# A state-space layer with a routed feed-forward block: moving sums, residual and rounding rest of a chunk from VectorE and GpSimd to TensorE and ScalarE, with new job orders

## The reference, cut to what matters

```
x = x + ssm(layernorm(x))
x = x + ffn(layernorm(x))
```

## Time and profile before

| | |
|---|---|
| median of three runs | 1964.43 us |
| lowest, highest | 1963.17, 1964.90 us |
| profiled execution, own time | 1968.13 us |
| its span, first to last instruction | 1966.3 us |
| VectorE busy | 1823.1 us (93%) |
| GpSimd busy | 1791.7 us (91%) |
| TensorE busy (matmuls) | 1628.6 us (83%) |
| ScalarE busy | 1431.6 us (73%) |
| mean granted clock of TensorE, share of full speed | 0.933 |

### The profile page before, as it was taken

One profiled execution on the slowest core, in us unless ns is written; L12 is line 12 of the kernel. 1 busy time (PEld: TensorE's weight loads), 2 busy tenths in 40 slices (PEclk: granted clock), 3 DMA queues, 4 the chain that ended last, 5 costly groups with the idle time before them and its releaser, 6 DMA issues.

```text
span 1966.3 us, 25727 instructions
## 1 busy us (share of the span) xinstructions
PE 1628.6 (83%) x6816; PEld 808.6 (41%) x6816; DVE 1823.1 (93%) x2246; ACT 1431.6 (73%) x2755; POOL 1791.7 (91%) x780
## 2 busy tenths in 40 slices
PE   3364779898898989889898988889898898988899
PEld 1111224444443444444344444444444444444456
DVE  2799999999999999999999999999999999999951
ACT  3566767877787777878777787877778787777643
POOL 1899999999999999999999999999999999999920
PEclk8666879999899999989999999999999999999999
DMA  4646553544646365464636536463643646265200
GB/s 167 142 112 155 119 138 90 142 123 92 161 111 155 91 152 123 96 151 112 161 84 149 126 92 152 112 165 79 158 118 94 148 111 166 68 156 118 58 14 19
DMA packets 146761, 234.92 MB, mean 119 GB/s; under 512 B 22064, under 2 KB 46896, under 8 KB 146096
## 3 DMA queue, kind: packets, MB, share of 16 engines
q1 hardware_dynamic: 146608, 233.18, 48.7%
HBM read 190.11 MB, written 42.99 MB: 119 GB/s over the span
## 4 chain that ended last, share of the span: by engine, by line
DVE 32%; POOL 23%; issue 17%; PE 17%; ACT 5%; DMA 1%; DVEq 0%; SPq 0%; POOLq 0%; ACTq 0%
POOL hs L1344 14%; DVE decay L1286 13%; DVE hs L1276 8%; DVE hs L1286 7%; POOL hs L1356 6%; PE bank L910 4%; PE bank L932 4%; ACT decay L1089 2%; PE y_ps L946 2%; POOL e_dt L1334 1%; DVE st L1146 1%; POOL z_dt L1323 1%; PE bank L894 1%; PE bank L914 1%; PE bank L884 1%
## 5 line engine op out<-in xcount | busy, mean ns | idle before, releaser
L1344 POOL TENSOR_TENSOR hs<-dx_rep,b_rep 128x2048 f32<-128x2048 f32 x256 | 1161.8, 4541 | 13.4 <-issue 11.1
L1286 DVE TENSOR_TENSOR_SCAN decay<-decay,state,hs 128x512 f32<-128x512 f32 x640 | 796.2, 1277 | 34.2 <-ACT decay L1089 27.4
L1089 ACT ACTIVATE decay<-dt_rep,a_sb 128x512 f32<-128x512 f32 x1024 | 690.0, 685 | 28.7 <-DMA dt_rep<-rep_scratch 10.3
L1286 DVE TENSOR_TENSOR_SCAN hs<-decay,state,hs 128x512 f32<-128x512 f32 x384 | 487.3, 1269 | 4.3 <-ACT decay L1089 3.7
L1356 POOL TENSOR_TENSOR hs<-hs,c_rep 128x1024 f32<-128x1024 f32 x192 | 453.6, 2362 | 6.3 <-ACT state L1103 6.3
L1276 DVE TENSOR_TENSOR hs<-decay,c_rep 128x1024 f32<-128x1024 f32 x320 | 385.1, 1204 | 0.0
L946 PE MATMUL y_ps<-hs,nsum 128*32 128x512 f32 x2048 | 290.3, 641 | 48.8 <-POOL hs L1356 30.6
L910 PE MATMUL bank<-w_i_sb,x_t 128*128 128x512 f32 x484 | 273.5, 693 | 28.9 <-DVE silu L1174 25.5
L868 PE MATMUL bank<-xn_t,w_in_sb 128*128 128x512 f32 x512 | 258.5, 635 | 14.5 <-ACT x_t L996 4.9
L1103 ACT COPY state<-decay 128x2 f32<-128x2 f32 x320 | 51.0, 159 | 266.8 <-DVE hs L1276 260.1
L932 PE MATMUL bank<-w_o_sb,r_t 128*128 128x256 f32 x944 | 224.1, 392 | 2.6 <-ACT r_t L1074 1.8
(11 more groups left out here) (163 smaller groups left out, 1747.7 us busy)
## 6 DMA issues: line engine op xcount, KB each, us to landing
dx_rep<-rep_scratch SPq DMA_DIRECT2D x256, 256.0 KB, 4.7
dt_rep<-rep_scratch SPq DMA_DIRECT2D x256, 256.0 KB, 7.6
b_rep<-bc_scratch SPq DMA_DIRECT2D x256, 64.0 KB, 3.9
rep_scratch<-z_dt SPq DMA_DIRECT2D x64, 256.0 KB, 2.5
rep_scratch<-e_dt SPq DMA_DIRECT2D x64, 256.0 KB, 2.7
c_rep<-bc_scratch SPq DMA_DIRECT2D x256, 64.0 KB, 2.6
xin<-in_u SPq DMA_DIRECT2D x16, 512.0 KB, 4.2
xr<-in_u SPq DMA_DIRECT2D x16, 512.0 KB, 4.3
```

The lines of the kernel that those rows point to most:

```text
L1089: nc.scalar.activation(decay[:, j, :], dt_rep[m % 2][:, j, :], ACT.Exp, scale=a_sb[:, J * s + j:J * s + j + 1]).then_inc(decay_ready, 1)
L1286: v.tensor_tensor_scan(hs[s % 4][:, j, :] if kept else decay[:, j, :], decay[:, j, :], hs[s % 4][:, j, :], state[:, b, n:n + 1], ALU.mult, ...
L1344: nc.gpsimd.tensor_tensor(hs[s % 4][:], dx_rep[m % 2][:], b_rep[:, k, :].unsqueeze(1).to_broadcast([P, J, T]), ALU.mult).then_inc(input_re ...
```

## The change

- The first residual is added by TensorE: F0 to F3 begin with a product of the identity with `xr` and add the product with W_out to it, except for the last chunk, which stays as it was. ScalarE copies the sum to x1 and gives the sum along each row by its accumulator output.
- The second layernorm's statistics are ScalarE's for all but the last chunk: P0 makes minus the mean, P1 and P2 square the centred tiles, two tiles each, with the accumulator output. R2 makes minus half of the variance, and the root. The squares themselves go to `xr` and are not used.
- dt's rest is made by TensorE: a product with minus the identity adds minus the rounded value to what is in the bank (C1 on TensorE), and ScalarE copies 64 rows of it to `dt_st` (C1 on ScalarE).
- GpSimd has no more layernorm jobs. VectorE runs A1 in three operations and O1, O2 in three each; R1 and R2 make the square of the root on ScalarE.
- All tables are new, with another place for many jobs, and in the first turn, before any scan, VectorE's N0, N1, A1, O1 stand together.

```diff
 PE_SIDE = [
-    "T0 late, S1 late, J2 late | J3 late, T1 late",
...
-    "B3 pre, S4 late, E1 main | ",
-    "C0 pre | J5 late, S5 late",
-    " | D0 pre, K1 late",
...
+    "J3 late, T1 late | S2 late",
...
+    "J5 late, C0 pre | K1 late",
+    "C1 pre | D0 pre, S5 late",
...
 ACT_SIDE = [
...
-    " |  | E0 main, V0 main | W0 main, Z0 main",
...
-    "C0 pre | J5 late | Q0 post, Q1 post | Q2 post, D0 pre",
...
+    " | F2 post, E0 main | V0 main, W0 main, Z0 main | ",
+    "F3 post | P0 post | T3 late, P1 post, B0 pre | B1 pre",
+    " | J4 late | B2 pre | B3 pre, S4 late, P2 post",
+    "R2 post | E1 main | V1 main, W1 main | Z1 main",
+    "J5 late, Q0 post | Q1 post, C0 pre | C1 pre | D0 pre",
...
+    "G0 post |  | G1 post, E2 main | T5 late, V2 main, W2 main, Z2 main",
...
 DVE_SIDE = [
-    "N0 pre, N1 pre |  |  | ",
-    " |  |  | Y3 post",
-    " |  |  | ",
-    "K0 late, F0 post |  |  | ",
-    " | F1 post | F2 post | S0 main",
-    "F3 post | P0 post |  | Y0 main",
-    " |  | P1 post | ",
-    " |  | S1 main | ",
-    "C0 pre |  | K1 late | ",
...
+    "N0 pre | N1 pre, A1 pre |  | ",
+    "O1 pre |  | K0 late, Y3 post | ",
+    " |  |  | ",
+    " |  |  | ",
+    " |  | S0 main | ",
+    " |  |  | Y0 main",
+    " |  |  | ",
+    "O2 post |  | S1 main | ",
+    " |  | K1 late | ",
...
 POOL_SIDE = [
-    "A1 pre, O1 pre",
+    "",
...
-    "A2 post",
-    "O2 post",
+    "",
+    "",
...
-        def center(eng, g, i, q):
-
+        def center(dve, i, q):
+
+            v = nc.vector
...
-            eng.wait_ge(part, 2 * (q + 1))
-            g.tensor_tensor(ve[:], mv[:, :, 1], consts[:, 0], ALU.add).then_inc(var, 1)
-            g.tensor_tensor(nw[:, 4], mv[:, :, 0], consts[:, 3], ALU.mult)
-            eng.wait_ge(var, q + 1)
-            g.tensor_tensor(nw[:, 3], ve[:], consts[:, 1], ALU.mult).then_inc(halved, 1)
+            dve.wait_ge(part, 2 * (q + 1) if i == 1 else 2)
+            v.tensor_scalar(ve[:], mv[:, :, 1], EPS, None, ALU.add).then_inc(var, 2)
+            v.tensor_scalar(nw[:, 3], mv[:, :, 1], EPS, -0.5, ALU.add, ALU.mult)
+            v.tensor_scalar(nw[:, 4], mv[:, :, 0], -1.0, None, ALU.mult).then_inc(halved, 1)
...
+        def newton(dve, i, q):
...
+            dve.wait_ge(halved, q + 1)
+            dve.wait_ge(root, 3 * (q + 1))
+            v.tensor_tensor(nw[:, 1], nw[:, 0], nw[:, 3], ALU.mult).then_inc(steps, 1)
+            dve.wait_ge(steps, NEWTON_STEPS * q + 1)
+            v.scalar_tensor_tensor(out=rs[:], in0=nw[:, 1], scalar=1.5, in1=rs[:], op0=ALU.add, op1=ALU.mult).then_inc(steps, 1)
+            dve.wait_ge(steps, NEWTON_STEPS * q + 2)
+            v.tensor_tensor(nt[:], nw[:, 4], rs[:], ALU.mult).then_inc(steps, 1)
...
             def job_pe(letter, i, when, job, c, par):
                 q, odd = chunk_of(c, when), odd_of(par, when)
+                if letter == "C" and i == 1:
+
+                    if isinstance(c, int) and c < 0:
+                        pe.wait_ge(weights_split, 1)
+                    pe.wait_ge(dt_hi, q + 1)
+                    pe.matmul(banks[used("C0", c, AHEAD[when])[0]][:], neg_id[:], dt_st[:], start=False, stop=True,
+                              skip_group_check=True).then_inc(dt_rest, 1)
+                    return
...
+                    if not is_last(q):
+                        if i == 0:
+                            pe.wait_ge(xr_loaded, 16 * (q + 1))
+                        pe.matmul(ps[:, cols], ident[:], xr[:, i, :], start=True, stop=False)
                     pe.wait_ge(gated_ready, M * q + ks[-1] + 1)
...
+                elif letter == "F":
+
+                    at_least(act, out_stored[i], 16 * (q - 1))
+                    ps, free = wait_filled(act, job[:2], c, when)
+                    nc.scalar.activation(x1[odd][:, i, :], ps[:, 0:D], ACT.Identity, accum_out=sum2[:, i:i + 1]).then_inc(free, 1)
+                elif letter == "P":
+                    if i == 0:
+                        wait_read(act, c, when, "F", range(TT))
+                        nc.scalar.mul(nw2[:, 4], sum2[:], -1.0 / D).then_inc(ln2_mean, 1)
+                    else:
+                        if i == 1:
+                            act.wait_ge(ln2_mean, q + 1)
+                        for t in (2 * i - 2, 2 * i - 1):
+                            last = nc.scalar.activation(xr[:, t, :], x1[odd][:, t, :], ACT.Square, bias=nw2[:, 4, t:t + 1],
+                                                        accum_out=sq2[:, t:t + 1])
+                        last.then_inc(ln2_var, 1)
+                elif letter == "C" and i == 1:
+                    act.wait_ge(dt_rest, q + 1)
+                    b, _ = used("C0", c, AHEAD[when])
+                    nc.scalar.activation(dt_st[64:128], banks[b][64:128], ACT.Identity,
+                                         bias=b_x_sb[64:128, 0:1]).then_inc(freed[b], 1)
...
-                    act.wait_ge(var, q + 1)
-                    nc.scalar.activation(rs[:], ve[:], ACT.Ln).then_inc(root, 1)
-                    act.wait_ge(root, 2 * q + 1)
+                    act.wait_ge(var, 2 * (q + 1))
+                    if by_vector(i, q):
+                        nc.scalar.activation(rs[:], ve[:], ACT.Ln).then_inc(root, 1)
+                    else:
+                        nc.scalar.activation(nw[:, 3], sq2[:], ACT.Identity, scale=-0.5 / D,
+                                             bias=consts[:, 4, 0:1]).then_inc(ln2_halved, 1)
+                        nc.scalar.activation(rs[:], sq2[:], ACT.Ln, scale=1.0 / D, bias=consts[:, 0, 0:1]).then_inc(root, 1)
+                    act.wait_ge(root, 3 * q + 1)
                     nc.scalar.activation(rs[:], rs[:], ACT.Exp, scale=-0.5).then_inc(root, 1)
+                    act.wait_ge(root, 3 * q + 2)
+                    nc.scalar.activation(nw[:, 0], rs[:], ACT.Square).then_inc(root, 1)
...
-                elif letter == "C":
-                    dve.wait_ge(dt_hi, q + 1)
-                    b, _ = used(job[:2], c, AHEAD[when])
-                    v.scalar_tensor_tensor(out=dt_st[64:128], in0=banks[b][64:128], scalar=b_x_sb[64:128, 0:1],
-                                           in1=dt_st[64:128].bitcast(F32), op0=ALU.add,
-                                           op1=ALU.subtract).then_inc(freed[b], 1)
```

More of the change, by code:

```diff
@@ L51 @@
 PE_SIDE = [
[16 rows of a table removed]
+    "J3 late, T1 late | S2 late",
+    "K0 late | S3 late, A0 pre",
+    "T2 late | F0 post",
+    "F1 post, F2 post, A1 pre | E0 main, F3 post, B0 pre",
+    " | T3 late",
+    "J4 late, B1 pre | B2 pre, B3 pre, S4 late",
+    "E1 main | ",
+    "J5 late, C0 pre | K1 late",
+    "C1 pre | D0 pre, S5 late",
+    "T4 late, E2 main | T5 late, D1 pre, G0 post, G1 post",
+    " | H0 post, J6 late",
+    "J7 late, S6 late | ",
+    "K2 late, S7 late | T6 late, E3 main",
+    "T7 late, I0 post | K3 late",
+    "J0 post, D2 pre | D3 pre, S0 post, J1 post",
+    "J2 post, S1 post | T0 post",
 ]
 ACT_SIDE = [
[16 rows of a table removed]
[16 rows of a table added]
 ]
 DVE_SIDE = [
[2 rows of a table removed]
[2 rows of a table added]
     " |  |  | ",
[12 rows of a table removed]
[12 rows of a table added]
     " |  |  | ",
@@ L137 @@
     "",
+    "",
     "K1 late",
+    "",
+    "K2 late",
     "",
@@ L142 @@
     "",
-    "K2 late",
-    "",
     "",
     "K3 late",
-    "",
 ]
 PE_LAST = [
-    "T0 late, S1 late | J2 late",
-    " | T1 late, E0 main",
-    "S2 late, F0 post, J3 late | K0 late",
-    "S3 late | T2 late, F1 post",
-    "F2 post | ",
-    "F3 post, T3 late, E1 main, J4 late | S4 late",
-    "K1 late, T4 late | ",
-    "J5 late | S5 late, T5 late",
-    "E2 main | ",
-    "G0 post | ",
-    "G1 post, J6 late, H0 post, S6 late, K2 late | ",
-    "J7 late | S7 late, T6 late, T7 late",
-    "K3 late | I0 post",
-    "E3 main, J0 post | S0 post, J1 post, T0 post",
-    "S1 post | T1 post, J2 post, K0 post",
-    " | S2 post",
+    "T1 late | ",
+    "J3 late, E0 main | ",
+    "S2 late, F0 post | ",
+    "K0 late, E1 main | S3 late, F1 post, F2 post, F3 post",
+    " | T2 late",
+    "T3 late | J4 late, K1 late",
+    "S4 late, T4 late | ",
+    "J5 late | S5 late",
+    "G0 post | E2 main",
+    "T5 late | G1 post",
+    "J6 late, H0 post, S6 late | K2 late, J7 late",
+    " | S7 late, T6 late, T7 late",
+    "K3 late, I0 post | J0 post, E3 main",
+    "S0 post, J1 post | S1 post",
+    "T0 post, T1 post | ",
+    "J2 post, K0 post, S2 post | ",
 ]
 ACT_LAST = [
[16 rows of a table removed]
[16 rows of a table added]
 ]
@@ L213 @@
     "",
+    "",
     "V1 main",
+    "U1 main",
     "",
-    "U1 main",
-    "A2 post",
-    "O2 post",
+    "",
     "",
@@ L327 @@
     "",
+    "",
 ]
 SP_END = [
+    "K1 late",
     "",
-    "K1 late",
+    "",
     "K2 late",
+    "K3 late",
     "",
@@ L339 @@
     "",
-    "",
-    "K3 late, K0 post",
-    "",
-    "K1 post",
+    "K0 post, K1 post",
     "",
@@ L370 @@
 AHEAD = {"pre": 1, "main": 0, "post": -1, "late": -2}
```

(21 more changed lines are left out.)

51 lines of the change are left out of this document (21 added, 30 removed), and 194 rows, old and new, of tables (ACT_END, ACT_LAST, ACT_SIDE, DVE_END).

## The result

The changed kernel takes 2203.70 us (median of four runs, 2200.48 to 2207.27) against 1964.18 of the kernel before (four runs): ratio 1.122, 95% interval 1.120 to 1.124. It is 12% slower. The prediction said 1935, with 1956 as the upper end and 2018 for its slower rival.

A forecast was written before the change was run, and what follows sets the result against it. VectorE was taken to set the pace of chunks 1 to 14. Profiled execution: 1968.1 - 33.2 (VectorE) - 1.0 (GpSimd, chunk 0) + 4.9 (new waits) = 1938.8; the median stands 3.7 lower, so 1935 us, range 1920 to 1956.

The forecast's parts named there:

- slower rival: ScalarE's decays come late for VectorE's scans: up to 6.2 us a chunk less 2.37 saved, 2018 us; chance 0.12.
- A Newton job: O1 or O2 on VectorE: three small operations priced from the tail at 0.48 us, 0.96 us for two.
- Removed from VectorE, 3.70 us a chunk: VectorE loses residual additions 1.32, second-layernorm statistics 1.30, aggregates 0.29 and dt's rest 0.79; net of 1.33 added, 2.37 us.
- New waits, 4.9 us: VectorE waiting longer before ScalarE's decays: 0.35 us a chunk over chunks 1 to 14.
- second rival: TensorE's chain delays sums, gates or D by 1.2 us a chunk, 17 us on top, 1952 us; chance 0.12.
- ScalarE's accumulator, 8 x 0.10: Accumulator output on ScalarE's copies and squares: 0.10 us each, 0.8 a chunk, on top of 0.49 us a tile.
- TensorE, 2.2 us a chunk: Four identity products, 1.55 us, and the product with minus the identity, 0.65, hidden in TensorE's 15 idle us.
- GpSimd, 3 us idle a chunk: GpSimd, rid of layernorm work, should idle some 3 us a chunk with its price unchanged and nobody waiting for it.
- the 5.4 named as the point: VectorE's waits before decays over two chunks: near 1.4 us fits the forecast, above 5.4 us makes the slower rival right.
- The two others: Whole durations set VectorE's price: 1926 us, chance 0.05; or new orders' waits eat what is freed: 1964 us, chance 0.05.
- Less than 97% busy in mid-chunk: Sign on VectorE: below 97% busy in mid-chunk, the prediction's mechanism is wrong, whatever the time.
- Start and tail: Both counted as no change in sum; the stretch from last scan to end should stay as long, with TensorE full.

The follow-up runs named there:

- The reverse move: The kernel before with only its two Newton jobs, O1 and O2, moved from GpSimd to VectorE; 2147.2 us, 1.092 of before.
- the form test: The changed kernel with three operation forms in each Newton job, part of the correction left out; run once for durations, its time not compared.
- e9_one_column_a1_scalare: The changed kernel with Newton in pointer form for one of four columns, the rest left out, and A1 moved to ScalarE; 1946.3 us, 0.9897 of before.
- e4_pointer_scalars: The pointer version: the changed kernel with each Newton operation done in four, a column at a time with a pointer scalar; 1956.5 us, 0.9952 of before.
- e6_one_column: The changed kernel with each Newton operation in pointer form for the first of four columns only, A1 left on VectorE; 1980.6 us, 1.0089 of before.
- e10_pointer_a1_scalare: The changed kernel with all Newton columns in pointer form and A1 moved to ScalarE, nothing left out; 1943.5 us, 0.9881 of before.

## Why the prediction was wrong

**What failed** is above all one step: "A Newton job is 0.20 + 0.20 + 0.08 = 0.48, two are 0.96." The durations were read from the earlier trace rows, in the tail, where GpSimd is idle. The trace before has no such operation in mid-kernel: there VectorE's small operations on two tensors have one in PSUM, and its others are statistics, reductions and a reciprocal, which are as short beside a busy GpSimd as elsewhere. Those that Newton needs were GpSimd's. So a price from a stretch with an idle neighbour was put into a chunk in which GpSimd is busy for 112.61 of 114 us, and the same prediction called that engine's load harmless since nobody waited for it. The real price is 18.4 us a chunk. Over the run the Newton and A1 groups above, with 2.8 us of L682, cover 288.6 us, and the removed 3.70 a chunk are 15 x 3.70 = 55.5: a difference of 233 us, where VectorE's busy time in the scans' stretch grew by 222.5 (a few of these operations stand ahead of it or behind it). The other 19.6 of the 242.1 are waits. The reverse move shows the loss without the rest of the change, the pointer version takes it away with nothing but the form changed, and the form test says which forms pay.

The bound of the unknown was also missing. Where the accumulator output had no row, the prediction gave it two ends; the same for a small operation beside a busy GpSimd would have given 0.16 us and the length of a GpSimd instruction, 4.54, for each of six operations: up to 27 us in a chunk. No rival had it. The Trainium skill, "GPSIMD Engine Reference", section "Specifications", lists the contention of GpSimd with VectorE's operations that have two SBUF inputs or use a mode with two ports; it speaks against this change, and the traces bear it out.

**Removed from VectorE, 3.70 us a chunk.** Right: in e9_one_column_a1_scalare VectorE's busy time while scans run fell by 45.2 us (1793.85 in 60 to 1885 us before, 1748.62 in 59 to 1865 there); the forecast's terms give 15 x (2.37 + 0.37) = 41, and with the measured 0.61 for a free Newton job 37. With pointer scalars nothing of it is left: two jobs of 1.70 and A1's 0.37 are 3.77, and e4_pointer_scalars is busy for 1798.4 us in this stretch. Its chunk fell from about 114 to about 113 us all the same, because VectorE is idle for 15.8 us of the stretch instead of 31.2: with a list as long as before, the new orders wait less than the old ones.

**New waits, 4.9 us.** Too small once the list is shorter. In e9_one_column_a1_scalare VectorE's idle time in this stretch grew from 31.2 to 57.4 us, by 26.2, over half of what the list had become shorter. (the earlier trace rows is also the fullest of three chunks: in those on either side of it VectorE is busy for 112.31 and 112.16 us.) Its time is 0.9897 of before, where the forecast was 0.985; 1946 lies between the forecast and its second rival (1952). So with all holds away, A1's too, the sign and the range of 1920 to 1956 would have held, and the size would have been ten us off; with A1 left on VectorE, e6_one_column, the time is above before (1.0089). As soon as VectorE is relieved by some 2.5 us in a chunk (3.70 less two jobs of 0.61), ScalarE and TensorE set the pace for part of a chunk: behind the first scan it waits 33.1 us before decays into `decay` where the kernel before had 7.2, and 14.6 us for the gate's product. e10_pointer_a1_scalare, with 2.2 us more on VectorE in a chunk, is no slower (0.9881).

**ScalarE's accumulator, 8 x 0.10.** Right in size, and its form is now known; the tile under it was priced too high. ScalarE in order of time, after:

```profile
1017.51 0.51 ACT L1034 ACTIVATE xr<-x,nw 128x256 f32<-128x256 f32 x1
1017.90 0.20 ACT L1034 ACTIVATION_READ_ACCUMULATOR xr<-x,nw 128x1 f32 x1
1018.00 0.50 ACT L1034 ACTIVATE xr<-x,nw 128x256 f32<-128x256 f32 x1
```

A square with its sum takes 0.49 us from start to start: 0.39, where the forecast had 0.49, and a second instruction of 0.10. A copy to x1 with its sum takes 0.36 (1006.42 to 1006.78 us). Together that is 3.4 us a chunk, where the forecast had 4.7. The squares start every 0.5 us as foretold.

**TensorE, 2.2 us a chunk.** The products that were added, 1000 to 1258 us, two chunks:

```profile
L904 PE MATMUL bank<-xr,ident 128*128 128x256 f32 x16 | 5.1, 398 | 0.0
L854 PE MATMUL bank<-dt_st,neg_id 128*128 128x512 f32 x2 | 1.2, 578 | 0.0
```

By busy time that is 3.2 us a chunk, one more than said, and neither group waited.

**GpSimd, 3 us idle a chunk.** It stands 20.3 us of 129 now, as its products wait for sums that are late with the scans; with the holds away it is 3.1 us of 113 (e4_pointer_scalars), as said. ScalarE, on which VectorE was to wait in the slower rival, waits itself for VectorE most of all:

```profile
ACT state L1155 <- DVE hs L1322: 308.4, 147, 10.5
ACT xin L1099 <- DVE nt L696: 102.8, 16, 7.6
```

**The rivals.** Late decays did not decide: 4.5 us before decays over two chunks in the changed kernel, under the 5.4 named as the point. The second rival came near in size once the holds were away; that TensorE's chain is what makes decays late there isn't shown. The two others were not what happened.

**The signs named.** "Less than 97% busy in mid-chunk" would not have caught it: VectorE was 97.7% busy (126.0 of 129) in a chunk that is 15 us too long. A held instruction counts as busy. The sign that tells is an instruction's duration against its shortest, or busy time against work. **Start and tail** went nearly as said, 1.6 and 1.3 us shorter.

## What to carry to other kernels

Before moving small operations to VectorE beside a busy GpSimd, ask of each form whether it reads two tensors from SBUF, or is a `tensor_scalar` from SBUF to SBUF over several fp32 elements (four here): such an operation takes not its 0.16 us but until GpSimd's instruction ends, 2.3 to 3.0 us in the mean. One element for each partition with a pointer scalar, an input from PSUM (as the scans have), or ScalarE is the way out; twelve free operations cost 1.7 us where three held ones cost 7.5 to 10.9. And a price is taken from a stretch in which the neighbours are as busy as in the place where the operation will stand.
